# Loading the edge features of a pair of quads in two halves of 64 partitions

## What is computed

```
h_s, h_v = node features @ lin1                      # per node
hid = silu(edge_attr_64 @ fc_w1 / 8)                 # per edge: the features that the change loads
w   = hid @ fc_w2 / 8                                # per edge, 224 weights
messages = products of w, h[src] and edge_attr_4     # per edge
agg = segment_sum(messages, dst)                     # per node
out = layernorm(x + gate(agg @ lin2 + x @ sc))       # per node
```

## Time and profile before

| | us |
|---|---|
| median of three runs | 4850.9 (4850.78 to 4855.17) |
| the profiled execution | 4850.68 |
| its span, first to last instruction | 4848.8 |
| PE busy | 4288.4 |
| POOL busy | 2993.6 |
| DVE busy | 2511.6 |
| ACT busy | 1978.0 |

### The profile page before, as it was taken

One profiled execution on the slowest core, in us unless ns is written; L12 is line 12 of the kernel. 1 busy time (PEld: TensorE's weight loads), 2 busy tenths in 40 slices (PEclk: granted clock), 3 DMA queues, 4 the chain that ended last, 5 costly groups with the idle time before them and its releaser, 6 DMA issues.

```text
span 4848.8 us, 66572 instructions
## 1 busy us (share of the span) xinstructions
PE 4288.4 (88%) x15455; PEld 1703.3 (35%) x15455; DVE 2511.6 (52%) x7621; ACT 1978.0 (41%) x5179; POOL 2993.6 (62%) x3136
## 2 busy tenths in 40 slices
PE   8888889888889898889888888988888888888887
PEld 6333333333333333333333333333333333333333
DVE  4455555555555555555555555555555555555554
ACT  3334444343434444444444443434343434444433
POOL 1666666666666666666666666666666666666663
PEclk9999999999999999999999999999999999999998
DMA  6433333333333333333333333333333333333332
GB/s 199 141 100 103 99 104 99 105 99 105 100 104 100 103 101 103 100 103 100 103 102 102 105 99 104 99 104 99 104 99 103 100 103 100 103 99 103 100 103 79
DMA packets 395010, 507.01 MB, mean 105 GB/s; under 512 B 71267, under 2 KB 277808, under 8 KB 394580
## 3 DMA queue, kind: packets, MB, share of 16 engines
q0 software_dynamic: 150000, 256.20, 21.5%
q1 hardware_dynamic: 172386, 133.82, 9.2%
q10 hardware_dynamic: 72578, 116.54, 8.4%
HBM read 426.23 MB, written 80.06 MB: 104 GB/s over the span
## 4 chain that ended last, share of the span: by engine, by line
another core or an unknown queue 40%; ACT 25%; PE 19%; issue 11%; ACTq 2%; DMA 0%; SPq 0%; DVE 0%; DVEq 0%
ACT aggsb L731 12%; ACT tsum L736 7%; PE psg L1013 5%; PE psg L1015 5%; PE psw L998 4%; PE pst_e L1005 3%; ACT hid L721 2%; ACT L721 2%; ACTq L709 1%; ACT L757 1%; PE psx L1028 1%; PE psx L989 1%; ACT turned L745 0%; ACT tanh_g L752 0%
## 5 line engine op out<-in xcount | busy, mean ns | idle before, releaser
L682 POOL DMA_INDIRECT rows<-h_table,src_cols x3125 | 2992.1, 957 | 1808.6 <-issue 934.0
L531 DVE TENSOR_TENSOR prod<-psw,rows 128x384 f32<-128x384 f32 (+2 forms) x3128 | 1211.0, 450 | 961.2 <-remote 504.9
L998 PE MATMUL psw<-fc,hid 128*128 128x480 f32 x3128 | 1476.9, 595 | 0.7 <-ACT hid L721 0.7
L731 ACT ACTIVATE aggsb<-psg 32x160 f32<-32x160 f32 x3128 | 917.7, 293 | 1371.7 <-remote 829.8
L1013 PE MATMUL psg<-tsum,shifts 128*128 128x448 f32 x1564 | 795.3, 591 | 398.6 <-ACT tsum L736 241.0
L998 PEld LDWEIGHTS psw<-fc,hid 128*128 128x128 f32 x3128 | 534.4, 191 | 940.0 <-issue 911.4
L1005 PE MATMUL pst_e<-prod,sel 128*32 128x448 f32 x6256 | 782.7, 573 | 2.0 <-issue 2.0
L1015 PE MATMUL psg<-tsum,shifts 128*128 128x448 f32 x1562 | 769.9, 576 | 0.0
L856 DVE TENSOR_TENSOR shifts<-shift,tile_offset 128x256 f32<-128x256 f32 x782 | 333.3, 426 | 731.1 <-remote 329.2
L989 PE MATMUL psx<-es,fc 128*128 128x512 f32 x782 | 419.6, 618 | 132.2 <-ACT turned L741 107.5
L1013 PEld LDWEIGHTS psg<-tsum,shifts 128*128 128x128 f32 x1564 | 247.8, 193 | 789.7 <-ACT tsum L736 493.5
(11 more groups left out here) (142 smaller groups left out, 1381.8 us busy)
## 6 DMA issues: line engine op xcount, KB each, us to landing
es<-in_esP ACTq DMA_DIRECT2D x391, 256.0 KB
agg_table<-aggsb SPq DMA_DIRECT2D x782, 80.0 KB
rows<-h_table,src_cols POOLq DMA_INDIRECT x3125
nag<-agg_table SPq DMA_DIRECT2D x96, 320.0 KB
h_table<-hrow ACTq DMA_DIRECT2D x24, 320.0 KB, 3.2
nxr<-in_x SPq DMA_DIRECT2D x96, 80.0 KB
out<-yn SPq DMA_DIRECT2D x95, 80.0 KB
xa<-in_xT SPq DMA_DIRECT2D x24, 256.0 KB, 2.6
```

The source lines that it names most:

```text
L531: return nc.vector.tensor_tensor(out, w_part, ev, ALU.mult)
L682: nc.gpsimd.indirect_dma_start(out=rows[:, u * QT + j, :], out_offset=None, in_=m.h, in_offset=bass.IndirectOffsetOnAxis(ap=m.src[:, t:t + ...
L731: ins = nc.scalar.activation(aggsb[r, b, :], picked(psg[r, :], k), ACT.Copy)
L998: ins = nc.tensor.matmul(both[:, 0:256 + WN], hid[:, at:at + P], m.fc2[:], start=True, stop=True)
```

## The change

The load of `es` becomes two DMAs of 64 partitions (128 KB) each. In the first quad of a pair, behind `activate`, ACT now issues only the half of partitions 0 to 63. The other half, partitions 64 to 127, is issued in the pair's second quad, behind `copy_tiles`. `hidden` waits for both (32 instead of 16 for each pair). The set-up and the place before the first round issue both halves in a row, and the end of the program leaves out the last one. Sizes, buffers, arithmetic and the order of everything else stay.

```
-            act.dma_start(m.es[:], io["esP"][:, 0:2 * CH]).then_inc(m.es_loaded, 16)
+            for h in range(2):
+                r = slice(S * h, S * h + S)
+                act.dma_start(m.es[r, :], io["esP"][r, 0:2 * CH]).then_inc(m.es_loaded, 16)
...
-            def load(r):
+            def load(r, h):
-                act.dma_start(es[:], io["esP"][:, ds(r * (2 * CH), 2 * CH)]).then_inc(es_loaded, 16)
+                half = slice(S * h, S * h + S)
+                act.dma_start(es[half, :], io["esP"][half, ds(r * (2 * CH), 2 * CH)]).then_inc(es_loaded, 16)
...
                 if following:
-                    load(r + 1)
+                    load(r + 1, 0)
...
                     copy_tiles(R * RING + u, b)
+                    if b == 1 and not (rest and u >= quads - 3):
+                        load(i + 2, 1)
...
                 activate(0, False, True)
+                load(1, 1)
...
-                pe.wait_ge(es_loaded, 16 * (r + 1))
+                pe.wait_ge(es_loaded, 32 * (r + 1))
```

More of the change, by code:

```diff
@@ L225, in _ @@
             sp.wait_ge(s_edge, 32)
-            sp.wait_ge(m.es_loaded, 16)
+            sp.wait_ge(m.es_loaded, 32)
         @block.gpsimd
```

## The result

The changed kernel takes **5338.7 us** (median of 4 runs, 5332.4 to 5363.1), the kernel before beside it 4853.0 us (4850.8 to 4859.2): ratio 1.1008, 95% interval 1.0979 to 1.1037. The forecast was 4970 us, in a range up to 5260: the sign was right, the size was short by 369 us.

The account below looks back on a forecast made before the run. It took POOL's own pace (3926 us) plus waits as the bound, with slack in POOL's pause. 4850.7 us plus 63 (u = 0 beyond its slack) plus 58 (lower clock) gave 4972, stated as 4970 us; range 4842 to 5260 us.

Parts of the forecast that it names:

- What bounds the kernel: POOL's own pace for 3926 us plus 875 us of waits; its pause after the second quad's sum is slack above 0.3 us.
- The split and its issue: The additional DMA issue on ACT's sequencer, 0.35 us per pair, is hidden; uncovered it would be 137 us.
- The landing: The late half lands 2.1 us after issue (2.0 to 2.6); `combine` then comes 3.5 us after the first `aggsb`.
- Against the slack, u = 0: In this pair the chain grows by 1.65 us against 1.0 us of slack: 0.65 us per round, 63 us in all.
- The clock: PE pauses before `hidden`; one stretch at the lower clock per round costs 0.6 us on average, 58 us in all.
- Against the slack, u = 2, 4, 6: In these pairs the chain grows by 1.3, 1.65 and 1.3 us against slack of 2.8, 2.8 and 2.55 us: all absorbed.
- The chain sets the pace: Rival: POOL's pause is no slack and each added microsecond on PE's chain shows, 572 us more, 5423 us; chance 0.13.
- The half is slow to land: Rival: the late half lands after 2.6 us, each pair's chain grows by another 0.5 us, 5080 to 5155 us; chance 0.1.
- Hidden anyway: Rival: in u = 0 the load leaves early and lands during PE's weights; within 10 us of 4851 us; chance 0.11.
- faster: Rival: a half-size burst brings POOL's last gathers forward, at most 196 us, so 4655 us; chance 0.05.
- only the last of the four pairs longer: Sign of the forecast: POOL's pause shrinks to 1.5 us for u = 2, 4, 6 and 0.3 us for u = 0.
- all four: Sign that the chain set the pace: all four pairs of a round longer, POOL's pause as it was.

Follow-up runs that it names:

- One copy of a matmul: Kernel before with the first matmul of `combine` issued once more in each pair's first quad, no DMA changed: 4891.8 us, 1.0077, on a chip of 4854 us.
- two buffers: Changed kernel with two `es` buffers, the second half issued at its late place for the pair after the next: 4931.7 us, 1.0183 of the kernel before.
- late whole load: Kernel before with all 128 partitions of `es` in one DMA at the place of the change's second half: 4619.1 us, 1.1296, on a chip of 4089 us.
- the wait without the bytes: Kernel before plus a late DMA of 64 partitions by 16 bytes that nobody reads but `hidden` waits for: 5208.1 us, 1.0634, on a chip of 4898 us.

## Why the prediction was wrong

**What bounds the kernel.** Right in the narrow form: the pause behind the second quad's sum is slack. One copy of a matmul took 0.7 us of it for 0.1 us. But the prediction took the pause for POOL's wait for `tiles_summed`, and moving that wait by a whole pair left it as it was. The prediction said that the profile doesn't tell what holds the increments back; it then used the pause as if only the last of them were held. One reading is off without touching the sum: of the 934 us that it gives to POOL's own pace, 100.4 us are a single stretch of set-up.

**The split and its issue.** Right as far as it was measured: 1.0015 for two halves at the old place, on a chip of 4089 us. An issue of 64 partitions takes 0.48 us instead of 0.34 us.

**The landing.** Mis-sized. Issue 0.30 us after the first `aggsb` (0.35 expected), then 2.64 us to `hidden` instead of 2.1 (u = 4: 3.23 us; SP loads node inputs at that time, and that these are the reason is not shown), then 0.96 us instead of 1.05 to `combine`: 3.96 us in u = 0, 4.81 in u = 4 (medians of all rounds) instead of 3.5. Counted from POOL's first gather, the end of the first quad's `combine` moved by 1.95, 1.18, 2.16 and 1.45 us for u = 0, 2, 4, 6 (medians at the full clock), where 1.65, 1.3, 1.65 and 1.3 stood. The nearest row would have been the 256 KB load, not the 106 KB one: the whole load takes 2.74 us at this place, the half 2.64 us. The Trainium skill's fit in "DMA: Bandwidth & Descriptors" (Anatomy of one DMA — SWDGE (gpsimd) path), 2.0 us plus the bytes over 436 GB/s, is given there for DMAs that GpSimd issues, and these are ACT's. It would have been nearer all the same: its 2.0 us is close to the 1.95 us of the DMA of 16 bytes a partition, and the estimate of 2.3 us from it for the half is still 0.3 us too low.

**Against the slack, u = 0.** Right in kind. The pair without a low-clock stretch went from 12.15 to 13.19 us, 1.04 us instead of 0.65, so 101 us instead of 63. Of the 0.39 us that were missed, 0.30 are the longer chain (1.95 instead of 1.65).

**The clock.** About right where it was binding: u = 0 had such a stretch in 28 of 94 rounds, 14.81 instead of 13.19 us, 45 us in all; before it was 6 rounds. The mean clock fell from 0.969 to 0.955. In u = 4 it was priced too low: 31 of 93 pairs had such a stretch and a `tsum` that was late by no more than 1.5 us, and they take 13.84 us instead of 12.17, 1.67 us per stretch, the longer landing of u = 4 with it, where 0.4 stood. That is another 52 us, so 97 instead of 58 us in all; in the pairs that are later than that, clock and lateness can't be taken apart.

**Against the slack, u = 2, 4, 6: the step that failed.** "1.65 of 2.8 ... All absorbed" looks at the second quad's sum alone. The first quad's sum is on the changed chain too, and it is now seen late: 265 of 295 pairs, by 1.8 us in the mean. PE then stands for `tsum` with most of the pair still to do. u = 0 has the node work of L1043 to cover that, u = 4 only the 0.60 us of L1028. Measured: 0.23, 2.69 and 0.77 us per round instead of 0, **358 of the 502 us**, some 50 of them the clock term just named. Two things make the sum seen late, each shown by a run: its place (one copy of a matmul, no DMA changed: 79 of 371 pairs) and the DMAs, by their number or by the late issue (two buffers, the sum's place unchanged: 114 of 300). Together, with a wait and hardly a byte, it is 263 of 317. That the lateness is what costs is shown in a single pair by the rows above. On average it rests on two comparisons. One is between pairs of the changed kernel itself: at the full clock 11.99 us where the `tsum` is late by up to 1.5 us, 14.16 us where it is late by over 3. The other is with the late whole load on the other kind of chip, where the chain is the same, nothing is late and the pairs of u = 2, 4 and 6 take 10.7 to 11.4 us, under the floor of about 12 us on the kind of the forecast. No run changed the lateness alone.

**The rivals.** "The chain sets the pace" (5423 us) is nearest in size, and not the mechanism: it needs every microsecond to show, and one copy of a matmul showed a seventh. "The half is slow to land" was true of the landing (2.64 us against its 2.6) and gave 5080 to 5155 us. "Hidden anyway" and "faster" fell: `hidden` waited in all 374 pairs.

**What was to be seen.** The idle time before `hidden` rose by 519 us (500 expected). That before `combine` fell from 398.6 to 283.3 us, and not to nearly nothing, as waits for `tsum` took its place. POOL's pause behind the modelled end shrank to 0.3 us in u = 0 as expected and to 1.4 us in u = 2 and 6 (medians; 1.5 was expected); in u = 4 it was 0.3 us too. The forecast named "only the last of the four pairs longer" or "all four": it was two, and a third in a part of the rounds.

## What to carry to other kernels

A pause is slack only for the event that was followed into it. A longer chain moves every increment on it, so for each one that another engine waits for, compare its modelled end with the start of the one who waits, not for the last alone. To find out whether a pause is a wait, move the wait's threshold: a run with it a pair earlier told more than any reading. And half a load took nearly as long as the whole when it was on the path: 2.64 against 2.74 us, so it has to be issued as early as the whole, and a second buffer is what made the late place cheap (1.018 instead of 1.098).

## What the runs showed of the hardware

- The same kernel takes 4087 to 4089 us on two of the chips and 4851 to 4898 us on others. A gather takes 0.96 us on both, with 0.30 us between two; the chips of 4087 to 4089 us have no pause of their own between the trains of eight gathers, and no `tsum` that is late by over 0.1 us.
- On the others some of PE's increments are seen up to 6.9 us after the modelled end (two buffers; 6.0 us in the changed kernel). In the pair shown of u = 4 the last gather ends at 2684.75 and the increment is seen at 2687.28; in 2.40 us between, no engine computes. The share of late ones was 5 of 300 pairs before, 79 of 371 with one copy of a matmul, 114 of 300 with two buffers, 263 of 317 with the wait without the bytes and 265 of 295 in the changed kernel. What holds them is open.
- A DMA from ACT's queue of 64 partitions by 16 bytes is waited out 1.95 us after its issue begins, one of 64 by 2 KB after 2.64 us, one of 128 by 2 KB after 2.74 us (medians of u = 0, the last on a chip of 4089 us). The issue takes 0.48 us for 64 partitions and 0.34 us for 128 (medians).
